# Seven block products for the output projection of a non-local block, taken as 2, 2 and 3 between pieces of the query projection

## The reference

```python
# x: (32, 1024, 32, 32) float32; theta, phi, g: 1024 -> 256; z: 256 -> 1024
q = einsum('bchw,dc->bdhw', x, theta_w) + theta_b          # b, 256, 1024
xpool = maxpool2(x)                                        # b, 1024, 16, 16
k = einsum('bchw,dc->bdhw', xpool, phi_w) + phi_b          # b, 256, 256
v = einsum('bchw,dc->bdhw', xpool, g_w) + g_b              # b, 256, 256
p = softmax(einsum('bdn,bdm->bnm', q, k) * 256 ** -0.5)    # b, 1024, 256
vp = einsum('bdm,bnm->bdn', v, p)                          # b, 256, 1024
out = einsum('bdhw,cd->bchw', vp, z_w) + z_b[...] + x
```

## Time and profile before

| | |
|---|---|
| median of 3 runs | 2207.38 us (2205.99 to 2208.12) |
| the profiled execution | 2208.27 us, its span 2206.5 us |
| PE busy | 2171.7 us, 98% of the span |
| DVE, ACT, POOL busy | 66%, 39%, 42% of the span |
| HBM read, written | 138.42 MB, 134.22 MB |
| granted TensorE clock | 0.995 of full speed in the mean |

### The profile page before, as it was taken

How to read it: one execution, slowest core, us unless ns; L and a number is a source line. 1 busy time by engine, 2 the same in 40 slices (tenths; PEclk the granted TensorE clock), 3 DMA queues, 4 the chain that set the end, 5 groups by cost and what they waited for, 6 DMA issues and landing times.

```text
span 2206.5 us, 32144 instructions
## 1 busy us (share of the span) xinstructions
PE 2171.7 (98%) x11520; PEld 1855.6 (84%) x11520; DVE 1466.0 (66%) x2355; ACT 852.1 (39%) x1521; POOL 918.0 (42%) x386
## 2 busy tenths in 40 slices
PE   6999999999999999999999999999999999999997
PEld 5788888888888888888888888888888888888885
DVE  7676666776666766667766667666677666676655
ACT  5344333344333443433433334434334333344331
POOL 4453343543434533435434345334354343443420
PEclk9999999999999999999999999999999999999999
DMA  6233334323234233343232342333433323423323
GB/s 229 77 113 117 119 113 149 135 104 142 100 128 152 107 121 116 113 152 130 108 143 95 133 152 105 124 114 114 152 125 112 140 98 133 152 105 124 114 77 114
DMA packets 143266, 272.91 MB, mean 124 GB/s; under 512 B 8592, under 2 KB 11664, under 8 KB 143248
## 3 DMA queue, kind: packets, MB, share of 16 engines
q1 hardware_dynamic: 143104, 272.66, 34.1%
q10 hardware_dynamic: 144, 0.01, 0.0%
HBM read 138.42 MB, written 134.22 MB: 124 GB/s over the span
## 4 chain that ended last, share of the span: by engine, by line
PE 96%; issue 1%; DVE 1%; ACT 1%; DMA 0%; POOL 0%; POOLq 0%; SPq 0%; ACTq 0%
PE bank L475 96%; DVE z_lo L356 0%; DVE pooled L365 0%; DMA x<-theta_wt 0%; DVE theta_lo L356 0%; POOL pt_lo L342 0%; ACT x_split_hi L244 0%; ACT q_hi L256 0%; POOLq L70 0%; ACT g_hi L237 0%; ACT pt_hi L315 0%; DVE xp_lo L417 0%; ACT xp_hi L248 0%; DVE att_lo L385 0%; DVE x L402 0%
## 5 line engine op out<-in xcount | busy, mean ns | idle before, releaser
L330 POOL TENSOR_TENSOR x_split_lo<-x,x_split_hi 128x1024 fp32r<-128x1024 f32 x256 | 617.5, 2423 | 872.6 <-ACT x_split_hi L244 869.8
L402 DVE SCALAR_TENSOR_TENSOR x<-bank,bias,x 128x512 f32<-128x512 f32 x512 | 383.2, 749 | 184.3 <-PE bank L475 184.1
L394 DVE STREAM_TRANSPOSE pt_raw<-probs 32x256 f32<-32x256 f32 x1024 | 446.8, 436 | 44.0 <-ACT probs L309 26.9
L475 PE MATMUL bank<-x_split_hi,theta_hi 128*128 128x512 f32 x1024 | 405.3, 396 | 10.3 <-POOL x_split_lo L330 10.3
L475 PE MATMUL bank<-x_split_lo,theta_hi 128*128 128x512 f32 x1024 | 409.9, 400 | 0.0
L475 PE MATMUL bank<-att_hi,z_hi 128*128 128x512 f32 x1024 | 405.4, 396 | 2.6 <-DVE att_lo L385 1.7
L475 PE MATMUL bank<-att_lo,z_hi 128*128 128x512 f32 x1024 | 405.5, 396 | 0.0
L475 PE MATMUL bank<-att_hi,z_lo 128*128 128x512 f32 x1024 | 405.1, 396 | 0.0
L475 PE MATMUL bank<-x_split_hi,theta_lo 128*128 128x512 f32 x1024 | 402.3, 393 | 0.0
L244 ACT ACTIVATE x_split_hi<-x 128x1024 fp32r<-128x1024 f32 x256 | 269.6, 1054 | 171.2 <-PE bank L475 166.7
L365 DVE TENSOR_REDUCE pooled<-x 128x256 f32<-128x1024 f32 x256 | 310.4, 1214 | 16.4 <-DMA x<-x 14.0
(11 more groups left out here) (51 smaller groups left out, 3420.7 us busy)
## 6 DMA issues: line engine op xcount, KB each, us to landing
x<-x SPq DMA_DIRECT2D x256, 512.0 KB, 5.6
out<-x SPq DMA_DIRECT2D x256, 512.0 KB, 2.8
x<-theta_wt SPq DMA_DIRECT2D x4, 256.0 KB, 7.1
x<-phi_wt SPq DMA_DIRECT2D x4, 256.0 KB, 10.1
x<-g_wt SPq DMA_DIRECT2D x4, 256.0 KB, 8.3
x<-z_wt SPq DMA_DIRECT2D x4, 256.0 KB, 7.1
bias<-biases ACTq DMA_DIRECT2D x1, 7.0 KB, 2.3
```

Of the source, the lines that this page charges most:

```text
L330: nc.gpsimd.tensor_tensor(xs[LO][:, ks, :], xb[s % BUFS][:, ks, :], raw(xs[HI][:, ks, :]), ALU.subtract).then_inc(x_ready, 1)
L394: last = nc.vector.transpose(dst, src)
L402: nc.vector.scalar_tensor_tensor(out=tile, in0=o_bank[i % 4][:, :], scalar=bias[:, Z_B + i:Z_B + i + 1], in1=tile, op0=ALU.add, op1=ALU.ad ...
L475: last = nc.tensor.matmul(dst, stationary(a), moving(b), start=start and n == 0, stop=stop and n == len(PRODUCTS) - 1)
```

## The change

The output projection is computed with 7 products of blocks in place of 8 (Strassen-Winograd). z is cut in 2 x 2 blocks (512 channels by 128), att in 2 x 2 blocks (128 by 256 pixels). Each of the 7 products is 4 tiles of 3 matmuls of 256 columns, 84 in all in place of 48 of 512 columns. The sums of blocks are made as follows:

- Four sums of z blocks are made once, in step 0 (`sum_z` on DVE, `split_z` on ACT, `lo_z` on DVE), and no longer before the first scores.
- Four differences of att blocks are made for each half on POOL (`blocks`, 256 elements in each partition each). ACT first copies att with its bias out of the banks (`copy_att`, 2 instructions), and makes three hi parts of 512, 768 and 512 elements (`hi_att`). POOL makes the three lo parts (`lo_att`); DVE no longer makes any.
- The sums of products are made partly in the banks, which stay open over several products, and partly by DVE in the residual tile: `add` has 14 instructions of 512 elements for each half, in place of 8. Some products wait for an `add` that reads the bank first (P6 for A_TOP, P7 for U_TOP, P3 for V_BOT, P4 for C22).
- The bias of z is added to the residual by ACT, 8 instructions for each half (`bias_top`, `bias_bot`).

x is loaded twice: once in chunks into 6 small buffers for the projection and the pooling, and once into `x_top` (2 buffers) and `x_bot` (1 buffer) for the residual. The split x has 3 chunk buffers in place of 4. The banks are shared in another way: k goes to bank 2, v to bank 6, the products to banks 2 to 7. `project_v` moves from the odd step's end to the even step, behind the scores. A loop of 6 steps is repeated 9 times, with steps 0, 1 and 56 to 63 around it.

```diff
+            def step(turn, s):                      # PE
+                scores(turn, s)
+                if begun(turn, s, 2):
+                    pe.wait_ge(o_added, upto(turn, s - 1, SUMS, 0))
+                if s % 2 == 0 and begun(turn, s, 1):
+                    project_v()
+                project_q(turn, s + 1, 0)
...
+                project_out(turn, s - 1, P1)
+                pe.wait_ge(exp_done, upto(turn, s, NT, NT))
+                project_out(turn, s - 1, P2)
+                project_q(turn, s + 1, 1)
+                project_out(turn, s - 1, P6)
+                project_out(turn, s - 1, P5)
+                project_q(turn, s + 1, 2)
+                project_out(turn, s - 1, P7)
+                project_out(turn, s - 1, P3)
+                project_out(turn, s - 1, P4)
+                project_q(turn, s + 1, 3)
+                if s % 2 and exists(turn, s, 1):
+                    pe.wait_ge(xp_ready, upto(turn, s, 1, 3))
+                    pe.wait_ge(o_added, upto(turn, s - 1, SUMS, 2 * C11 + 1))
                     project_k()
+                attend(turn, s)
```

The odd and the even step of ACT, the odd step of DVE, and POOL (all new):

```diff
+            def step_even(turn, s):                 # ACT
+                exps(turn, s)
+                normalize(turn, s)
+                hi_v(image_of(turn, s))
+                if behind:
+                    hi_att(turn, s - 1, 1)
+                    hi_att(turn, s - 1, 2)
...
+                if more:
+                    hi_q(turn, s + 1)
+                if next_x:
+                    hi_x(turn, s + 2, 2)
+                    hi_pooled(turn, s + 2, pooled[:, :, :])
...
+                copy_att(turn, s)
+                hi_att(turn, s, 0)
+
+            def step_odd(turn, s):                  # ACT
+                exps(turn, s)
+                hi_att(turn, s - 1, 1)
+                normalize(turn, s)
+                hi_att(turn, s - 1, 2)
...
+                if more:
+                    hi_q(turn, s + 1)
+                if next_x:
+                    hi_x(turn, s + 2, 2)
+                hi_pt(turn, s)
+                if more:
                     hi_k(image_of(turn, s, 1))
+                copy_att(turn, s)
+                hi_att(turn, s, 0)
...
+            def step_odd(turn, s):                  # DVE
+                max_scores(turn, s)
+                pool_ahead(turn, s, 0)
+                invert(turn, s)
+                pool_ahead(turn, s, 1)
+                add(turn, s - 1, A_TOP)
+                transpose_probs(turn, s, 0)
+                pool_ahead(turn, s, 2)
+                pool_ahead(turn, s, 3)
+                add(turn, s - 1, U_TOP)
+                transpose_probs(turn, s, 1)
+                add(turn, s - 1, C11)
+                add(turn, s - 1, V_BOT)
+                transpose_probs(turn, s, 2)
+                add(turn, s - 1, C22)
+                transpose_probs(turn, s, 3)
+                add(turn, s - 1, C12)
...
+            def blocks(turn, s):                    # POOL
+                pool.wait_ge(att_copied, upto(turn, s, DT, DT))
+                difference(T1, B12, B11)
+                pool.wait_ge(t_done, upto(turn, s, 4, 1))
+                difference(T2, B22, T1)
+                lo_att(turn, s, 0)
+                pool.wait_ge(t_done, upto(turn, s, 4, 2))
+                difference(T4, T2, B21)
+                difference(T3, B22, B12)
...
+            def step(turn, s):                      # POOL
+                if begun(turn, s, 1):
+                    lo_att(turn, s - 1, 1)
+                    lo_att(turn, s - 1, 2)
+                if more:
+                    lo_x(turn, s + 1, 3)
+                if next_x:
+                    lo_x(turn, s + 2, 0)
+                    if s % 2:
+                        lo_pooled(turn, s + 2)
+                        lo_x(turn, s + 2, 1)
+                        lo_x(turn, s + 2, 2)
+                lo_pt(turn, s)
+                if next_x and s % 2 == 0:
+                    lo_x(turn, s + 2, 1)
+                    lo_x(turn, s + 2, 2)
+                    lo_pooled(turn, s + 2)
+                blocks(turn, s)
```

More of the change, by code:

```diff
@@ L53 @@
 PRODUCTS = ((HI, HI), (HI, LO), (LO, HI))
+HB = H // 2
+TB = KT // 2
+A11, A12, S4, A22N, S1, S2, S3 = range(7)
+B11, B21, T3, B22, T1, T2, T4 = range(7)
+B12 = T3
+SPLITS = ((B11, T3), (T1, T4 + 1), (T3, T1))
+P1, P2, P6, P5, P7, P3, P4 = range(7)
+A_TOP, U_TOP, C11, V_BOT, C22, C12, C21 = range(7)
+SUMS = 14
 def non_local_block(nc, x, theta_wt, phi_wt, g_wt, z_wt, biases, out):
@@ L209, in _ @@
[L209 to L221, removed]
@@ L231, in _ @@
+            load_bot(TURNS, last)
+            store(TURNS, last)
+            for j in range(2):
+                sp.wait_ge(top_stored[j], IMAGES * 32)
+                sp.wait_ge(bot_stored[j], HALVES * 16)
         @block.scalar
@@ L327, in lo_x @@
             def lo_x(turn, s, c):
-                ks = slice(c * KC, (c + 1) * KC)
                 pool.wait_ge(x_hi, upto(turn, s, CH, c + 1))
[L330 to L340, removed]
+                if begun(turn, s, 2):
+                    pool.wait_ge(pooled_done, upto(turn, s, CH, c + 1))
@@ new lines, in _ @@
+            for c in range(CH):
+                lo_x(0, 0, c)
+            lo_pooled(0, 0)
+            for c in range(3):
+                lo_x(0, 1, c)
+            def step(turn, s):
+                more, next_x = exists(turn, s, 1), exists(turn, s, 2)
+                if begun(turn, s, 1):
+                    lo_att(turn, s - 1, 1)
+                    lo_att(turn, s - 1, 2)
+                if more:
+                    lo_x(turn, s + 1, 3)
+                if next_x:
+                    lo_x(turn, s + 2, 0)
[9 more added lines that the diff above has]
+                blocks(turn, s)
@@ L466, in _, with step, product @@
+            def step(turn, s):
+                if not begun(turn, s, 1):
+                    step_first(turn, s)
+                else:
+                    (step_even, step_odd)[s % 2](turn, s)
             steps(dve, step)
-            lo_att(TURNS, BUFS - 1)
-            finish(TURNS, BUFS - 1, range(KT))
+            last = FIRST + PERIOD + PERIOD // 3 - 1
+            for which in range(7):
+                add(TURNS, last, which)
         @block.tensor
         def _(pe):
-            def product(dst, stationary, moving, start, stop):
+            def product(dst, stationary, moving, start, stop, reopens=False):
```

534 lines of the change are left out of this document (348 added, 186 removed).

## The result

The changed kernel takes 2302.82 us in the median of 4 runs (2301.76 to 2302.97), the kernel before 2207.45. The ratio is 1.0432, with a 95% interval of 1.0414 to 1.0450. The forecast was slower, 2257 us, with a range to 2300. The direction was right, and the time lies 2.8 us outside the range. The profiled execution has a span of 2301.2 us, 94.7 more than before.

The account below looks back on a forecast made before the run. PE alone was taken to bound the middle. The old span of 2206.5 us plus 31 (middle), 13 (start) and 5 (end) gave 2255.5, taken as 2257 us for the measured time, range 2195 to 2300.

Parts of the forecast that it names:

- the sum for the middle: 31 pairs of steps: PE's 65.1 us plus three stalls makes 68.5 a pair, 1.0 more than before, +31 us.
- Rival C: Odd steps: PE's clock falls to half rate for 3 us after the stalls, 1.5 us each, 2304 us; chance 0.12.
- TensorE's part: Output projection on PE: 84 matmuls of 256 columns take 10.0 us in place of 11.19, gaining 2.4 a pair.
- The three waits: PE stalls in odd steps: 1.18 us for pt_lo, 0.93 before the first product, 1.3 before the fourth.
- POOL's chain: Around odd scores: lo_x, lo_pooled, two block differences and a lo part end at 6.5 us, delaying the first product.
- Even steps: Steps where project_v covers 5.7 us more ahead of the first product: no stall, least margin 1 us.
- loads: Second load of x: DMA share rises from 0.34 to about 0.5, hidden with some 3 us to spare.
- The start: Before scores of half 1: z's sums and seven lo parts on DVE delay lo_q, +13 us in all.
- The rule on two SBUF inputs: DVE instructions with two SBUF inputs contend with POOL's SBUF reads, others don't; the 14 adds keep their price.
- The end: Last attention and output projection: block differences, lo part and a wait for lo parts give 50 for 44.6, +5 us.
- A: No change: POOL's chain finishes before the first product is due, a pair takes 66.8, 2204 us; chance 0.12.
- B: Faster: PE stays the bound, stalls under 1.8 us a pair; 2151 at none, 2204 at half; chance 0.14.

Follow-up runs that it names:

- e1: The changed kernel without any loop, all 64 steps written out for every engine: 2243.31 us, ratio 1.0165 to the kernel before.
- f1: The changed kernel without a loop, hi and lo parts of pooled x made ahead of the last x chunk in even steps: 2190.40 us, ratio 0.9924.

## Why the prediction was wrong in its size, point by point

**The step that failed** is "65.1 + 1.18 + 0.93 + 1.3 = 68.5 a pair", the sum for the middle. It takes all 31 pairs as alike, as the pairs before were, and has no term for the jump back of a loop that grew from 4 steps to 6. That term is 57 us by e1, 8 jumps of 7.1. Rival C came to nearly the measured time, 2304, by luck: it had the clock falling in each odd step. In the middle it falls only behind the 8 jumps, and that is some 2.5 of the 7.1 us of each. The page of the kernel before had a sign that I didn't follow, its 0.18 MB of instructions for 15 turns.

**TensorE's part.** Mis-sized. 84 matmuls were put at 10.0 us from the scores' and k's rates. The timeline shows 36 of them in 4.09:

```profile
276.01 0.28 PE L748 MATMUL bank<-att_hi,z_hi 128*128 128x256 f32 x1
...
280.10 0.39 PE L748 MATMUL bank<-x_split_hi,theta_hi 128*128 128x512 f32 x1
```

That is 0.1136 each, 9.5 a step, below the lower bound taken. A pair without waits is 64.1 us, 3.4 less than before and not 2.4 (32.05 + 32.05, by the window of half 6).

**The three waits.** Right in place, order and cause, each shown by its own experiment. Their sum was 3.4 and is 4.1. The two errors nearly cancel, which is luck: an ordinary pair was forecast at 68.5 and is 68.2. Without a loop the kernel takes 2243, 14 below the forecast. POOL's chain runs as walked (timeline of POOL, start and duration, the odd scores begin at 1063.33):

```profile
1062.44 2.42 POOL L494 TENSOR_TENSOR x_split_lo<-x,x_split_hi 128x1024 fp32r<-128x1024 f32 x1 [4.80 <-ACT x_split_hi L320]
1064.81 2.41 POOL L499 TENSOR_TENSOR xp_lo<-pooled,xp_hi 128x1024 fp32r<-128x1024 f32 x1
1067.17 1.57 POOL L507 TENSOR_TENSOR att_f<-att_f 128x256 f32<-128x256 f32 x2
1068.69 1.27 POOL L512 TENSOR_TENSOR att_lo<-att_f,att_hi 128x512 fp32r<-128x512 f32 x1
```

It ends 6.6 after the scores' start; 6.5 was forecast. The differences took 0.74 and not 0.6 to 0.7. P4's wait is 1.5 in place of 1.3, since PE's shorter blocks ahead of it make it due 0.3 earlier. ACT's hi part then waits 2.5 us for the next difference with the scaling queued behind it, and DVE has no gap up to C22:

```profile
1070.68 0.85 ACT L359 ACTIVATE att_hi<-att_f 128x768 fp32r<-128x768 f32 x1 [2.54 <-POOL att_f L507]
1071.44 1.69 ACT L408 ACTIVATE probs<-probs,rowinv 128x256 f32<-128x256 f32 x4
```

```profile
1073.16 1.77 DVE L597 STREAM_TRANSPOSE pt_raw<-probs 32x256 f32<-32x256 f32 x4 [0.77 <-ACT probs L408]
...
1084.69 1.29 DVE L615 TENSOR_TENSOR x_bot<-bank,x_bot 128x512 f32<-128x512 f32 x2
```

C22 starts 21.36 after the scores; 21.26 was forecast.

**Even steps** without waits and **loads** hidden: right. x is read twice (272.64 MB in place of 138.42), and no wait of the middle goes to a DMA.

**The start.** +11.2 for +13. The seven lo parts of z took 10.4 us for 11.5 forecast, the first three of them 7.91 beside POOL's instructions:

```profile
69.03 7.91 DVE L636 SCALAR_TENSOR_TENSOR z_lo<-x_bot,z_hi 128x512 fp32r<-128x512 f32 x3
76.86 2.48 DVE L636 SCALAR_TENSOR_TENSOR z_lo<-att_f,z_hi 128x512 fp32r<-128x512 f32 x4
```

The rule on two SBUF inputs that the prediction cites (Trainium skill, SBUF — State Buffer, Who interferes with whom) holds here, and so does its other half: 570 adds that lie beside POOL's instructions took 0.68, and so did 120 that don't. (The prediction names rows 7 for adds beside POOL, but POOL is idle there. The trace of the kernel before has 185 adds beside POOL, at 0.75, the same as the others.) **The end.** +6.1 for +5, right.

**Rivals.** A and B fell: the waits were there, and POOL's chain set the one at P1 and part of the one at P4 (f1). The Trainium skill (TensorE: Matmul & The Clock Gate, A second HAM failure mode: psum-queue depth-cycling) tells of a kernel that such short idle times throttled repeatedly. Carried over to this kernel that is C, and it didn't come: the clock kept 1.00 through three waits of 0.9 to 1.4 us in each odd step.

## What to carry to other kernels

When a change makes a loop's body longer, count each engine's instructions in it, not only the time: here PE's body of 1440 matmuls and weight loads was not fetched again, 2160 and more were fetched anew at each jump back, and the row of the instruction queue tells which it is. A dependency walk with durations from the old trace found three waits of about a microsecond within 0.3 us each, and also how to remove them: an instruction that waits for the newest data belongs behind those that don't, on every in-order queue. The saving in matmuls was real (3.4 us a pair), and became visible only when those orders and the loop were mended.

## What was not expected of the hardware

- A jump back to code that wasn't kept cost PE 0.9 to 4.8 us of idle time, depending on the kernel and on the turn. In the changed kernel (3.8 to 4.8 us idle) the matmuls behind it ran at half rate for some 5 us.
- Matmuls of 256 columns of the block products come every 0.1136 us, those of the scores every 0.1196, though both have a weight load each. Why isn't known.
- Short POOL instructions with two SBUF inputs took 0.74 us at 256 elements, 1.28 at 512, 1.85 at 768 and 2.41 at 1024: a fixed part near 0.18, where a MEMSET of one element had shown 0.1.
